# A two-layer attention and feed-forward kernel: query and key rows stacked by one transfer per head and part, other pieces between the attention steps

## The reference, cut to what matters

```python
x = x + attn0(norm(x)) + ffn0(norm(x))   # 16 heads of 32, rope, causal; 512 -> 2048 -> 512, silu gated
x = x + attn1(norm(x)) + ffn1(norm(x))   # the same attention; 512 -> 1408 -> 512, scales on the weights
```

## Time and profile before

| | |
|---|---|
| median of three runs | 2057.23 us |
| profiled execution, its own time | 2055.59 us |
| its span, first to last instruction | 2053.8 us |
| TensorE busy, matmuls | 1866.4 us (91%), 8656 instructions |
| VectorE busy | 1116.6 us (54%) |
| ScalarE busy | 1060.1 us (52%) |
| GpSimd busy | 703.4 us (34%) |
| mean granted TensorE clock | 0.958 |

### The profile page before, as it was taken

The page is one execution under the profiler, slowest core; times in us unless marked ns, Lnnn a source line. Parts: engine busy times, 40 slices in busy tenths (PEclk is TensorE's granted clock), DMA queues, the critical chain, the costliest instruction groups (busy, mean ns, idle before and its releaser), DMA issues.

```text
span 2053.8 us, 25605 instructions
## 1 busy us (share of the span) xinstructions
PE 1866.4 (91%) x8656; PEld 1347.6 (66%) x8656; DVE 1116.6 (54%) x2432; ACT 1060.1 (52%) x2353; POOL 703.4 (34%) x516
## 2 busy tenths in 40 slices
PE   4999999999899899898889999999988998998987
PEld 3777767775675666656467777776757756575654
DVE  6554647373755564736346465573746636455452
ACT  2464646556256473646425646464652555646363
POOL 3225243242341533333213243534314415233320
PEclk9999999999999899999779999999999999999989
DMA  4213113031130313103213131311401403121201
GB/s 159 67 42 98 42 44 90 27 99 41 52 88 22 87 47 73 42 21 109 72 62 78 37 92 42 84 56 29 122 11 52 101 9 98 42 68 37 66 7 41
DMA packets 59874, 126.20 MB, mean 61 GB/s; under 512 B 9440, under 2 KB 10464, under 8 KB 58720
## 3 DMA queue, kind: packets, MB, share of 16 engines
q1 hardware_dynamic: 59744, 124.57, 22.0%
HBM read 69.48 MB, written 4.19 MB: 36 GB/s over the span
## 4 chain that ended last, share of the span: by engine, by line
PE 69%; DVE 11%; ACT 6%; SPq 5%; issue 5%; POOL 3%; DMA 2%; DVEq 0%; ACTq 0%; POOLq 0%
PE D L905 15%; PE G L905 11%; PE U L905 8%; PE OE L999 7%; PE SS L983 6%; PE OE L905 6%; PE SS L905 6%; SPq L564 5%; PE OE L983 3%; PE OE L962 3%; PE SS L962 2%; DVE OE L826 2%; ACT OE L618 2%; ACT pr L634 2%; DMA QS<-pr 1%
## 5 line engine op out<-in xcount | busy, mean ns | idle before, releaser
L874 DVE TENSOR_TENSOR xres<-D,xres 128x512 f32<-128x512 f32 x352 | 243.1, 691 | 214.1 <-PE D L905 209.7
L634 ACT ACTIVATE pr<-SS 128x512 f32<-128x512 f32 (+3 forms) x512 | 232.2, 501 | 143.8 <-PE SS L983 135.5
L709 POOL TENSOR_TENSOR hl<-tt,hh 128x512 fp32r<-128x512 f32 x108 | 139.0, 1287 | 475.7 <-ACT hh L651 475.7
L618 ACT ACTIVATE OE<-OE,mp 128x384 f32<-128x384 f32 (+3 forms) x256 | 203.4, 795 | 104.9 <-DVE mp L826 104.0
L826 DVE CUSTOM_DVE_ANT_0 OE<-OE,mask 128x384 f32<-128x384 f32 (+3 forms) x256 | 220.5, 873 | 50.6 <-PE OE L962 49.7
L618 ACT ACTIVATE SS<-SS,mp 128x128 f32<-128x128 f32 (+3 forms) x256 | 162.2, 634 | 95.7 <-DVE mp L826 94.0
L728 POOL TENSOR_SCALAR_AFFINE_SELECT pr<-pr 128x512 f32<-128x512 f32 x128 | 81.0, 635 | 378.7 <-ACT pr L634 378.7
L826 DVE CUSTOM_DVE_ANT_0 SS<-SS,mask 128x128 f32<-128x128 f32 (+3 forms) x256 | 167.6, 673 | 64.3 <-PE SS L962 63.0
L905 PE MATMUL G<-xh,wgh 128*128 128x512 f32 x432 | 178.0, 412 | 24.0 <-DVE tt L885 22.8
L983 PE MATMUL SS<-QS,KS 98*128 98x512 f32 (+2 forms) x512 | 182.1, 413 | 14.9 <-ACT pr L634 12.3
L905 PE MATMUL D<-wdh,hh 128*128 128x512 f32 x432 | 174.2, 403 | 19.6 <-DVE xres L874 13.7
(11 more groups left out here) (123 smaller groups left out, 3733.6 us busy)
## 6 DMA issues: line engine op xcount, KB each, us to landing
KS<-pr SPq DMA_DIRECT2D x192, 128.0 KB, 2.3
QS<-pr SPq DMA_DIRECT2D x192, 128.0 KB, 2.3
raw<-in_wgate_dram SPq DMA_DIRECT2D x27, 512.0 KB, 3.7
raw<-in_wup_dram SPq DMA_DIRECT2D x27, 512.0 KB, 3.7
raw<-in_wdown_dram SPq DMA_DIRECT2D x27, 512.0 KB, 3.7
raw<-in_wqk_dram SPq DMA_DIRECT2D x16, 512.0 KB, 4.4
val<-in_x_dram SPq DMA_DIRECT2D x4, 1024.0 KB, 6.9
trig<-in_wv_dram SPq DMA_DIRECT2D x4, 1024.0 KB, 5.6
```

What stands on the lines that cost most here:

```text
L618: act.activation(s, s, ACT.Exp, bias=mp[:, c, at:at + 1], scale=-1.0, accum_out=se[:, c, at:at + 1]) \
L634: act.activation(weights(i)[:, h, skip:W], SB[(i * HG + h) % 3][:, skip:W], ACT.Exp, scale=-1.0) \
L709: pool.tensor_tensor(hl[:, fc, :], tt[:, (blk * nfc + fc) % 2, :], hh[:, fc, :].bitcast(F32), ALU.subtract) \
L874: dve.tensor_tensor(xres[:, rt, :], d[:, :], xres[:, rt, :], ALU.add).then_inc(sem["v_dfree"], 1)
```

## The change

- **Stacks.** The flat buffers become `parts`, one tile of three rows side by side (high, again, low) for each projection. ScalarE writes the high part twice. SyncE then copies each head's 32 partitions x 3 rows into 96 partitions with one transfer of 192 KB, as soon as one projection is rotated: 4 transfers for each of the four projections, 16 a turn instead of 24. Row 3p + j of a stack is part j of row p.
- **Order.** The projections go k first half, q first half, k second half, q second half. The first `nat` steps wait for the first two only, and the 17th waits for the rest (`d_later`). In the opening three of the `values` move ahead of the last two projections.
- **Pieces.** `GU_PARTS = 3`: gate and up pieces of 4 matmuls. All strings of `PACE` are new.
- **Border.** `v_weights` comes after the second norm step instead of ahead of `xn`; the order of rows, statistics and norms stays as it is. `keep` becomes a transfer from x in DRAM, issued by SyncE. The statistics' short-lived values lie in PSUM.
- **Start.** The first 512 rows come in four transfers of one tile each, and ahead of the constants. The splits of the first down, gate and up weights (`first`) come after the first norms.
- **GpSimd** splits weights in operations of 512 columns instead of 1024 or 2048.
- The first two operations of the logarithm's guess go from VectorE to one on ScalarE; some waits are made only where they are needed.

```diff
-GU_PARTS = 2
+GU_PARTS = 3
@@ plan, normal, opening, START
-    return [("stats", layer, 0)] + [("v_weights", 1)] * layer + [("xn", layer, 0), ("xn", layer, 1)]
+    return [("stats", layer, 0), ("xn", layer, 0), ("xn", layer, 1)]
...
+        items[-3].append(("v_weights", 1))
...
-    out += [values[4], ("rotate", 0), proj[1], values[5], ("rotate", 1), proj[2], values[6], ("rotate", 2), proj[3], values[7],
+    out += [values[4], ("rotate", 0), proj[1], values[5], values[6], values[7], ("rotate", 1), proj[2], ("rotate", 2), proj[3],
...
-START = [("row", 0, rt) for rt in range(TPC)] + [("stats", 0, 0), ("v_weights", 0), ("xn", 0, 0), ("xn", 0, 1)]
-START += [x for piece in norms(0, range(TPC)) for x in piece] + [("keep", 0)]
+START = [("row", 0, rt) for rt in range(TPC)] + normal(0)
+START += [("v_weights", 0)] + [x for piece in norms(0, range(TPC)) for x in piece] + [("first",), ("keep", 0)]
@@ PACE, the strings of batch 0: layer 0 turns 2 and 4, layer 1 turns 2 and 3
-         "00700010101001100112021102021111111020010020010000100100000100100001000010010000010010001001000000000",
+         "00100020010012000212021211111113021020010110100000160010000100100001000010010000010010000011000000000",
...
-         "007000101010011001120212010211111110200100200000000000000000000000000000000000000000000000006021"),
+         "00200011010110012013030202111212021020010010020000130010000101000001000010010000010010000011z030"),
...
-         "00300010010011001103021021111111111011001001000000100100000000000000000000000000000000000000000000000",
+         "00200030001000100113031212111112121020021001000000100010000100200001000010100000000000000000000000000",
-         "00700010101010011012021202112111111000000000000000000000000000000000000000000000000000000000000000000",
+         "00400020010002000204031111021112112011101101000000100010000100100001000010010000000000000000000000000",
@@ sync: the first rows, keep, the stacks
+            for rt in range(TPC):
+                sp.dma_start(val[:, rt, :], x[0, rt * P:(rt + 1) * P, :]).then_inc(d_tile[rt], 16)
...
+            def keep(n, c):
+                sp.wait_ge(sem["d_out"], n("d_out"))
+                sp.dma_start(xres[:, c * TPC:(c + 1) * TPC, :], rows(x, n, c, n.batches)).then_inc(sem[f"d_keep{c}"], 16)
...
             def rotate(n, t):
-                if t % NC < NC - 1:
-                    return
-                qk = t // NC
-                flats = ((flat_h, flat_h, flat_l), (flat_h, flat_l, flat_h))[qk]
+                qk, c = t % 2, t // 2
+                cols = slice(c * W, (c + 1) * W)
                 sp.wait_ge(sem["g_rl"], n("g_rl", 1))
+                sp.wait_ge(sem["a_rh"], n("a_rh", 2))
                 if qk:
                     sp.wait_ge(sem["p_v"], n("p_v"))
                 for h in range(HG):
-                    for r, src in enumerate(flats):
-                        at = slice(r * DH, (r + 1) * DH)
-                        sp.dma_start((QS[at, :, h, :] if qk else KS[at, h, :]).bitcast(F32),
-                                     src[qk][h * DH:(h + 1) * DH, :]).then_inc(sem[f"d_stack{h}"], 16)
+                    sp.dma_start((QS[0:STACK, c, h, :] if qk else KS[0:STACK, h, cols]).bitcast(F32),
+                                 parts[t][h * DH:(h + 1) * DH, :, :]).then_inc(sem["d_later" if c else f"d_stack{h}"], 16)
@@ gpsimd
             def low(kind, src):
                 hi, lo = SPLIT_TO[kind]
-                return pool.tensor_tensor(flat(lo), src[:, 0:SIZE[kind]], flat(hi).bitcast(F32), ALU.subtract)
+                for at in range(0, SIZE[kind], W):
+                    part = slice(at, at + W)
+                    ins = pool.tensor_tensor(flat(lo)[:, part], src[:, part], flat(hi)[:, part].bitcast(F32), ALU.subtract)
+                return ins
@@ tensor, nat
+                if t < 4:
+                    held = 1 if n.turns == 0 else 3
+                    pe.wait_ge(sem["v_swap"], n("v_swap", min(0, t - held)))
...
                 elif t == HG * TPC:
+                    pe.wait_ge(sem["d_later"], n("d_later"))
```

More of the change, by code:

```diff
@@ L54 @@
 RING = 4
-GU_PARTS = 2
+TILES = True
+DIGITS = "0123456789abcdefghijklmnopqrstuvwxyzABCDEFGHIJKLMNOPQRSTUVWXYZ"
+GU_PARTS = 3
 SIZES = ((2,) * 8, (1,) + (2,) * 5)
@@ L199, in plan @@
         g1, d1 = ([[x for x in p if x[0] != "w"] for p in q] for q in (g1, d1))
-    pieces += g0[:GU_PARTS] + late + g0[GU_PARTS:] + g1[:GU_PARTS]
+    pieces += g0[:3] + late + g0[3:] + g1[:3]
     if l == 0:
@@ L203, in plan @@
         rows[-1] += normal(1)
-        pieces += rows + g1[GU_PARTS:] + output(1) + [piece + [("row", 1, TPC + i)] for i, piece in enumerate(d1)]
+        pieces += rows + g1[3:] + output(1) + [piece + [("row", 1, TPC + i)] for i, piece in enumerate(d1)]
         items += norms(1, range(TPC))
+        items[-3].append(("v_weights", 1))
     else:
@@ L281 @@
     "row": {"v_row": 1},
+    "first": {},
     "stats": {"v_chain": 13},
-    "keep": {"a_keep": 1},
+    "keep": {},
     "x_next": {"d_x0": 16, "d_x1": 16},
@@ L336, in __init__ @@
         self.first = dict(self.n)
+        self.batches = 0
+        self.written = {}
         self.w_ready = {k: CREDIT["g_lo"] + 1 + i for i, k in enumerate(SPLITS_OPEN)}
@@ L342, in dk, with fresh, close @@
         return (self.d - 1) % 2
+    def fresh(self, rt):
+        return self.b not in self.written.get(rt, {})
+    def close(self, rt):
+        return self.written.get(rt, {}).get(self.b, 0) > self.n["v_dfree"] - 1
     def scaled(self, slot):
@@ L367, in did @@
             self.b, self.layer = step[1:]
+        if step[0] == "keep":
+            self.n[f"d_keep{step[1]}"] += 16
+        if step[0] == "x_next":
+            self.batches += 1
+        if step[0] in ("add_wo", "add_down"):
+            rt = step[1] * TPC + step[2]
+            self.written.setdefault(rt, {})[self.b] = self.n["v_dfree"] + 1
         if step[0] == "turn":
@@ L485, in two_layers @@
         d_first = {k: ctx.enter_context(nc.semaphore(f"d_first_{k}")) for k in SPLITS_OPEN[1:]}
+        d_tile = [ctx.enter_context(nc.semaphore(f"d_tile{rt}")) for rt in range(TPC)]
         def load(sp, kind, at, dst, done):
@@ L750, in row @@
             def row(n, layer, rt):
-                if layer == 0:
-                    dve.wait_ge(sem[f"d_x{rt // TPC}"], n(f"d_x{rt // TPC}", 16))
+                if layer == 0 and rt < TPC and n.batches == 0:
+                    dve.wait_ge(d_tile[rt], 16)
+                elif layer == 0:
+                    c = rt // TPC
+                    dve.wait_ge(sem[f"d_x{c}"], n(f"d_x{c}", 16 * c))
                 else:
@@ L889, in gated @@
                     .then_inc(sem["v_h"], 1)
-            walk(dict(v_weights=v_weights, row=row, stats=stats, xn=xn_, norm=norm, proj=proj, rotate=rotate, nat=nat, guess=guess, better=better, log=log_, flip=flip, heads=heads_, add_wo=add_wo, add_down=add_down, gated=gated))
+            walk(dict(v_weights=v_weights, row=row, stats=stats, xn=xn_, norm=norm, proj=proj, rotate=rotate, nat=nat, better=better, log=log_, flip=flip, heads=heads_, add_wo=add_wo, add_down=add_down, gated=gated))
         @block.tensor
```

165 lines of the change are left out of this document (84 added, 81 removed).

## The result

The changed kernel takes 2000.95 us (median of 4 runs, 1999.46 to 2003.13) against 2057.74 for the kernel before on the same chip: ratio 0.973, 95% interval 0.9704 to 0.9757. It is faster, but by 57 us where 129 were forecast, and 1928 as well as the range 1888 to 1985 missed it. The profiled execution took 2002.15 us, its span is 2000.4 us and its mean granted clock 0.965.

The account below looks back on a forecast made before the run. TensorE was taken to bound the kernel, with gains where it waits or crawls behind ScalarE or VectorE. Terms -78 - 20 - 14 - 10 - 8 = -130 on 2055.6 us gave 1925.6, written as 1928; 80% range 1888 to 1985.

Parts of the forecast that it names:

- The wait for the stacks: Ahead of each turn's first `nat`: 5.0 us behind the projections instead of 13.4, bounds 3.0 and 13.2; 0.9 us a transfer.
- (3): Stacks come no earlier: the wait stays 13.2 us with its cover gone, 98 us back, 2026 us; chance 0.06.
- (4): Slower: transfers over 96 partitions slow in themselves; at 2.0 us each, 168 us more, 2096 us; chance 0.05.
- The first half of `nat`: First 16 `nat` steps of a turn: some 12.5 us, the earlier trace's row, with the new filling of pieces.
- Pieces in the sets of layer 1: About 8 us of pieces a turn move to sets with TensorE room; layer 1's eight stretches fall from 726.9 to 649, -78.
- Rival (1): Pieces are not free in the sets: layer 1 gives back 30 us, layer 0 its 20, 1978 us; chance 0.20.
- Behind the last sets of layer 0: Turn 4's last sets take pieces for -10 us a pass; the border into layer 1 gives 7 us each, -14 for two.
- Border between batches: ScalarE's 7.5 us wait for the store and its 1.9 us copy go: -10 us, bounds -4 and -14.
- start: Kernel start: fewer delays beside GpSimd operations, first projection at 27 us instead of 35; -8 us, bounds -3 and -13.
- GpSimd's halves: GpSimd's smaller weight splits shorten one wait but leave as many, so nothing was counted for them alone.

Follow-up runs that it names:

- The experiments with order: Changed kernel with the last rotation behind the fourth `nat` (1979.94 us), the next q and k weights' split behind the eighth (1987.9 us), or both (1977.46 us).
- kernel with the late rotation: Changed kernel with each turn's last rotation behind the fourth `nat` step instead of ahead of the first: 1979.94 us, ratio 0.962.
- kernels with an operation more: Late last rotation as base (1979.94 us), with the second copy made twice on ScalarE (1988.36 us) or an extra add on VectorE (1992.26 us).
- the shift rows above: Late last rotation as base (1979.94 us), one piece in layer 1's turn 1 moved just behind the shift rows' step: 1970.22 us, ratio 0.9579.

## Why the prediction was wrong, and where it was right

The sum missed by 76 us (1925.6 against the 2002.15 of the profiled execution). In the order of the prediction:

- **The wait for the stacks: right.** First `nat` 4.6 to 5.2 us behind the projections in five of the six later turns of batch 0 (6.0 in the sixth), for 5.0 forecast, and no wait ahead of the 17th. A transfer takes 0.72 to 0.75 us instead of 0.90, and rivals (3) and (4) are out.
- **The first half of `nat`: the step that failed.** The prediction took 12.5 us for it from the earlier trace rows, "with that filling", as if a phase cost what its matmuls cost. That row held while the queues of ScalarE and VectorE came into it empty. It takes 15.0 to 17.7 us in layer 1 and 12.0 to 17.2 in layer 0, 244.3 us over the 16 turns. The prediction's prices (13, 12.5, 12.5 and 11.5 in layer 1, 12 to 12.5 in layer 0) make 195 to 199: 45 to 49 of the 76 us. The experiments with order give back 25 of the 52.6 us that it takes beside the pieces, so that about half is shown to be order. The cause of the other 28 is open. The kernel with the late rotation still idles 17.5 us in these phases, against 1 before, and the kernels with an operation more show that added work of either engine costs there a half to all of its length; that the 28 us are such work (the rotation, copies and split that had run in the wait) is inferred from that and not shown by taking them away. The rival is the clock: the new strings alone lengthen these phases by 42 us with nothing moved into them. Against it: in the kernel after at most 2.2 us of idle time lie ahead of the first `nat`, not 8, and turns with none have the low clock too (0.90, 0.89 and 0.77 in turns 1, 3 and 4 of layer 1), so that it follows idle time inside the phase. No run parts the two.
- **Pieces in the sets of layer 1: right.** Last eight sets with pieces, and those of layer 0's turn 4 (26.5 and 29.8 forecast, as their base):

```profile
854.30:880.00 25.70, 24.76 (x141) 14.92 (x139) 7.55 (x11) 15.57 (x35) 3.86 (x6) 1.00 0.00 1
448.60:477.50 28.90, 28.90 (x176) 18.96 (x176) 7.50 (x11) 16.90 (x37) 4.63 (x7) 1.00 0.00 1
```

  7 and 12 us of pieces cost 1 to 1.5 us, at full clock (the empty rows had 0.93 and 0.88, so that the clock gives back a part). Rival (1) gave 1978, some 24 us from the result like rival (3), but by a mechanism that did not occur. The one row of the sets that is off is turn 1's first sets (16.9 for 12.4), the shift rows above, 9 us over both batches. In the second half of `nat` turn 1 took 37.9 us for 33.7 and turn 2 29.6 for 32.5; over all of layer 1 that phase is 4 us above its forecast.
- **Behind the last sets of layer 0: half of what was forecast.** From the last sets of turn 4 to the next pass, -17 was forecast for each pass through layer 0 and -10.0 and -6.1 came, beside the pieces; 18 us of the miss. The pieces of the `z` ran near full rate, not at it: 154 matmuls in 38.5 us, where 35 us would do. The waits of TensorE from 477 to 540 us name GpSimd's low part for a down piece (2.6), the `xn` (2.2) and a weight split (1.6); over the run the first is the 12.5 us of the group of L940 above. The `xn` pair itself was read rightly: 1.00 us at 516.38, against 5.18 in the earlier trace rows, and VectorE's copy of the value weights runs behind it:

```profile
477.50:516.00 38.50, 35.49 (x154) 28.37 (x152) 16.28 (x36) 7.81 (x11) 12.70 (x10) 1.00 0.13 41
...
516.38 1.00 DVE L826 TENSOR_SCALAR pr<-xres,mv,st 128x512 f32<-128x512 f32 x2
...
522.03 1.22 DVE L785 CAST QS<-trig 128x2048 fp32r<-128x2048 f32 x1
```

  How the 18 us divide was not tried.
- **Border between batches -10, start -8: right within 3 us** (-7.4 and -8.4).
- **GpSimd's halves at nothing: right**, by the kernel with whole splits.
- Two slips in the working change nothing in the sum. By the prediction's own list 5.9, 2.3, 5.9 and 5.9 us of pieces leave the cover of the stacks, 5 us a turn and not 8. And at 2.0 us a transfer, by its own times, head 0 of q would land at 309.1, 5.1 us later than 304.0 and not 4.5.

The sign was right. The range missed because no rival held the loss that came: "the work that lies under the wait comes back behind it". It could have been priced as one rotation of VectorE and, on ScalarE, two copies and a split for each group of heads; with the durations above that is 1.7 and 2.3 us, 16 times, an estimate of up to 64 us, in which the clock is not counted.

## What to carry to other kernels

When a wait is shortened, list what other engines did during it: it doesn't vanish, it now stands in their in-order queues ahead of the next phase's first steps. Move back what is needed latest (here a rotation that only the 17th score needs), and look in each queue for what the critical item now stands behind. A phase's duration from the profile is a price only with the same state of all queues, and the same clock, at its start.

## What the runs showed of the hardware

- Transfers of 192 KB from 32 to 96 partitions followed each other at 0.72 to 0.75 us, 255 GB/s over the stretch below, where those of 128 KB from 32 to 32 did at 0.63, with 212 GB/s over theirs, at the same DMA share of 0.94:

```profile
794.00:800.00 6.00, 3.10 (x10) 2.26 (x11) 3.10 (x10) 4.32 (x10) 4.62 (x4) 0.78 0.94 255
```

  The Trainium skill, "SBUF — State Buffer", in its part on the DMA port swizzle, would hold a transfer from 32 partitions to some 218 GB/s. The 255 GB/s of this stretch are above it. The four heads' transfers read four different groups of 32 partitions and can overlap, and each writes 96; which of the two matters was not tried.
- Idle TensorE time cost more here than its length: 2.9 us of it were followed by some 3 us of matmuls at 1.2 GHz. With the new strings alone, waits of 8.2 us in the mean (10.8 at most) put the clock of the first half of `nat` behind them at 0.70 to 0.87, and the mean of the whole execution at 0.937, against 0.958 before and 0.965 after.
